# A fused attention and mixture-of-experts block on one Trainium2 core: the expert part rebuilt around one-hot bias matmuls, rows kept in place and pieces copied whole

## The reference

```python
x = x + xcond(layernorm(x), ctx, ctx, tau, delta, Wq, bq, Wk, bk, Wv, bv, Wo, bo)
# the FFN of the layernorm of that x:
logits = x @ router_w + router_b;  top1 = argmax(softmax(logits))
for i in range(8):
    h = x @ w1[i] + b1[i]                 # 256 -> 2 * 1024
    a, g = split(h, 2)
    y = (a * sigmoid(g)) @ w2[i] + b2[i]  # 1024 -> 256
    out = out + where(top1 == i, y, 0)
x = x + out
```

## Time and profile before

| | |
|---|---|
| three timed runs | 442.26, 443.79, 444.25 us; median 443.79 us |
| span of the profiled execution, first to last instruction | 441.3 us |
| the profiled execution's own time | no other than the span is shown; the median lies 2.5 us above it |
| TensorE matmul busy | 390.7 us (89%) |
| vector engine, ScalarE, GpSimd busy | 275.3, 236.1, 156.4 us |
| attention up to the routing | 0 to about 187 us |
| expert part | 207.4 us to the end |

### The profile page before, as it was taken

The page is one execution under the profiler, slowest core; times in us unless marked ns, Lnnn a source line. Parts: engine busy times, 40 slices in busy tenths (PEclk is TensorE's granted clock), DMA queues, the critical chain, the costliest instruction groups (busy, mean ns, idle before and its releaser), DMA issues.

```text
span 441.3 us, 8739 instructions
## 1 busy us (share of the span) xinstructions
PE 390.7 (89%) x2905; PEld 267.0 (61%) x2913; DVE 275.3 (62%) x734; ACT 236.1 (54%) x433; POOL 156.4 (35%) x195
## 2 busy tenths in 40 slices
PE   6959889898998889969887779989999999999990
PEld 3535444455564455735565667767697668968870
DVE  3859975577675754773635655476656567458750
ACT  3215567456465466103476775566675557657640
POOL 5349050011010010346776732142222235057742
PEclk9989999899998899996999998999999999999996
DMA  6655595261011562043785630393106911021311
GB/s 216 118 163 118 116 177 183 54 143 51 3 49 50 180 253 97 30 169 102 268 260 202 233 121 24 126 394 127 25 24 244 376 28 25 25 61 62 95 61 36
DMA packets 27042, 56.12 MB, mean 127 GB/s; under 512 B 6930, under 2 KB 17174, under 8 KB 26870
## 3 DMA queue, kind: packets, MB, share of 16 engines
q1 hardware_dynamic: 20954, 41.41, 29.7%
q0 software_dynamic: 4528, 13.16, 9.7%
q10 hardware_dynamic: 1516, 0.99, 1.0%
HBM read 41.23 MB, written 6.88 MB: 109 GB/s over the span
## 4 chain that ended last, share of the span: by engine, by line
PE 65%; DVE 11%; ACT 6%; issue 6%; DMA 5%; ACTq 1%; SPq 1%; POOL 1%; another core or an unknown queue 1%; DVEq 0%; POOLq 0%
PE bank L1242 17%; PE bank L1270 8%; PE bank L1235 7%; PE bank L1264 4%; PE bank L1082 4%; PE bank L1005 4%; DMA bias_in<-b_rows,bias_row 3%; PE bank L995 3%; DVE row_max L1601 3%; PE bank L944 2%; PE bank L905 2%; PE bank L881 2%; PE bank L1057 2%; PE bank L983 2%; ACT probs L1355 2%
## 5 line engine op out<-in xcount | busy, mean ns | idle before, releaser
L1242 PEld LDWEIGHTS bank<-slot_xt,w_now 128*128 128x128 f32 x832 | 100.4, 192 | 5.1 <-issue 2.0
L1242 PE MATMUL bank<-slot_xt,w_now 128*128 128x128 f32 x832 | 101.1, 275 | 2.1 <-issue 1.5
L826 POOL COPY piece_w<-w_sb 128x1024 f32 x30 | 31.6, 1060 | 97.4 <-PE bank L1235 97.3
L1601 DVE TENSOR_REDUCE row_max<-bank 128x3 f32<-128x462 f32 (+1 forms) x96 | 52.8, 579 | 17.0 <-PE bank L944 16.7
L1871 DVE SCALAR_TENSOR_TENSOR act_ut<-bank,b_of,gate 128x128 f32<-128x128 f32 x104 | 31.6, 346 | 50.0 <-ACT gate L1473 46.5
L1355 ACT ACTIVATE probs<-bank 128x512 f32<-128x512 f32 x80 | 45.9, 598 | 25.9 <-PE bank L983 17.0
L1445 ACT ACTIVATE w_now<-w_sb 128x1024 f32 x52 | 54.6, 1053 | 9.4 <-issue 9.3
L1270 PE MATMUL bank<-w_sb,act_ut 128*128 x208 | 55.2, 389 | 0.5 <-issue 0.5
L693 POOL TENSOR_SCALAR var<-mv 128x1 f32<-128x1 f32 (+1 forms) x20 | 4.5, 226 | 133.4 <-DVE mv L1638 109.5
L1901 DVE COPY piece_w<-w_sb 128x512 f32 x80 | 51.0, 658 | 1.3 <-issue 0.7
L1457 ACT ACTIVATE piece_w<-w_sb 128x1024 f32 x44 | 45.9, 1051 | 2.3 <-issue 2.3
(11 more groups left out here) (188 smaller groups left out, 575.9 us busy)
## 6 DMA issues: line engine op xcount, KB each, us to landing
w_sb<-in_weights_dram SPq DMA_DIRECT2D x32, 768.0 KB, 7.1
q_stack<-q_split SPq DMA_DIRECT2D x18, 256.0 KB, 5.2
rows<-row_buf SPq DMA_DIRECT2D x17, 256.0 KB, 2.2
x_sb<-in_x_dram SPq DMA_DIRECT2D x4, 512.0 KB, 6.2
b_sb<-in_b_dram SPq DMA_DIRECT2D x1, 1024.0 KB, 8.3
k_stack<-k_split SPq DMA_DIRECT2D x12, 77.0 KB
q_stack<-q_split ACTq DMA_DIRECT2D x6, 128.0 KB, 2.9
q_stack<-q_split SPq DMA_DIRECT2D x6, 128.0 KB, 2.7
```

Of the source, the lines that this page charges most:

```text
L1242: ins = pe.matmul(h_ps[j % RING][:, P * m:P * (m + 1)], w1_now[:, whole_count(n) % 2, k, P * m:P * (m + 1)], slot_xt[:, tile_at(n), k, :], ...
L1601: dve.tensor_reduce(row_max[:, c % 2, m, t, first:first + k], score_bank(c, i)[:, 0:k * CTX].rearrange("p (h s) -> p h s", s=CTX), AX_X, A ...
```

## The change

- Mixed tiles stand at 2, 5, 8, 11, 14, and the `down` of a mixed tile runs three steps after its `up`.
- b1 and b2 are split into three bf16 parts (`split_biases`, GpSimd, at step (0, 8)), stored and loaded back as `b_split`, 24 rows (3 parts x 8 experts). A one-hot `of_tile` picks the expert. Each mixed `up` begins with four bf16 matmuls of 24 rows x 32 columns x 512; in the first quarter each whole `down` begins with one of 24 x 128 x 256, and each mixed `down` with four of 24 x 32 x 256. The bias add on the vector engine, the gathers of b1 and b2 rows, `start_y`, `hidden`, `y_acc` and the 1 MB broadcast of b2 go.
- The transpose of b1 that feeds the split is moved from after the attention to step (0, 4) of TensorE (`turn_b1`), its copy to (0, 6) of ScalarE; `turn_x(3)` also waits for the copy.
- All 18 row gathers are issued one after another into `slot_rows`, where the turned rows are written back over the gathered ones and the outputs add up.
- Mixed pieces are copied whole, w1 and w2 together (1536 columns), into one of two sets: two by the vector engine, one by ScalarE, one by GpSimd, from three steps before their tile. A set is free when the mixed tile two back has had its `down`.
- The whole tiles' b1 columns of a quarter are placed by one masked product and one sum on the vector engine (`place_b1`), one quarter before the loop, three at steps 6, 9 and 12.

```diff
-MIXED_AT = (3, 6, 9, 12, 15)
+MIXED_AT = (2, 5, 8, 11, 14)
+MIXED_LAG = 3
+TURN_B1, SPLIT_BIASES = (0, 4), (0, 8)
...
+            def load_biases():
+                sp.wait_ge(pv_done, UNITS * CHUNKS)
+                sp.wait_ge(bias_stored, 32)
+                for w in range(PARTS):
...
             load_q(2)
             load_k(1)
             sp.dma_start(b1_sb[:, :, :], b1.rearrange("p (e m) -> p e m", m=HIDDEN_BLOCKS)).then_inc(s_b1, 16)
+            sp.dma_start(biases[:, P:], b2.rearrange("(p n) -> p n", p=P)).then_inc(s_b2, 16)
...
+            def turn_b1():
+                pe.wait_ge(s_b1, 16)
+                pe.wait_ge(q_low, KD)
+                pe.transpose(work_ps[0][:, 0:P], b1_sb[:, :, :].rearrange("p e m -> p (e m)"), ident).then_inc(b1_turned, 1)
...
+                if (c, i) == TURN_B1:
+                    turn_b1()
                 if c + 1 < CHUNKS:
                     scores(c + 1, i)
...
+            pool.wait_ge(tables_done, 1)
+            copy_piece(0)
             pool.wait_ge(routed, 1)
...
-            for j in range(GATHERS):
+            for j in range(SLOT_TILES):
                 gather(j)
+                if j == 5:
+                    copy_piece(1)
...
+                    for c in range(PIECES):
+                        pe.matmul(h_ps[j % RING][PIECE * c:PIECE * (c + 1), :], expert_rows(piece_at(k_mixed, c), PIECE),
+                                  b_split[:, 2 * HQ * q:2 * HQ * (q + 1)], start=True, stop=False, skip_group_check=True)
...
+                    if first:
+                        pe.matmul(y_ps[d % RING][:, 0:DIM], expert_rows(tile_at(n), P), b2_rows, start=True, stop=False)
...
+            def copy_piece(k, c):
+                at = piece_at(k, c)
+                wait_piece(dve, k)
+                if k < MIXED_TILES:
                     load_expert(at)
+                dve.tensor_copy(piece_w[:, k % 2, c, :], piece_weights(k, experts[at])).then_inc(pieces_dve, 1)
```

More of the change, by code:

```diff
@@ L99 @@
 BUSY_BEFORE_REST, BUSY_BEFORE_ROOMS, BUSY_BEFORE_FFN = 10, 2, 18
-GATHERS = 4
 RING = 3
@@ L328, in build @@
         zeros_stored = sem("zeros_stored")
-        gathered = [sem(f"gathered{n}") for n in range(GATHERS)]
+        gathered = [sem(f"gathered{n}") for n in range(SLOT_TILES)]
         s_out = sem("s_out")
@@ L466, in whole_at @@
             return [i for i in range(QUARTERS * SLOT_TILES) if not mixed(i)][w]
[L468 to L472, removed]
         def downs(n):
-            first = [last_mixed(n)] if mixed(n) and last_mixed(n) is not None else []
+            first = [n - MIXED_LAG] if n >= MIXED_LAG and mixed(n - MIXED_LAG) else []
             return first, [n - 2] if n >= 2 and not mixed(n - 2) else []
@@ L480, in build, with pieces_due, piece_at, wait_piece @@
         down_order = sum((sum(downs(n), []) for n in range(steps_all)), [])
-        down_order += [last_mixed(steps_all), steps_all - 2, steps_all - 1]
+        down_order += [steps_all - 2, steps_all - 1]
         def downs_before(n):
             return down_order.index(n)
[L487 to L510, removed]
+        def pieces_due(n, lag):
+            k = mixed_count(n - lag) if n >= lag and mixed(n - lag) else 0
+            return [k] if 2 <= k < QUARTERS * MIXED_TILES else []
+        def piece_at(k, c):
+            return WHOLE_TILES + PIECES * (k % MIXED_TILES) + c
+        def wait_piece(engine, k):
+            engine.wait_ge(s_quarter[k // MIXED_TILES], 16 * EXPERTS)
+            if k == 1:
+                engine.wait_ge(rest_ready, 1)
+            if k >= 2:
+                engine.wait_ge(y_ready, downs_before(mixed_at(k - 2)) + 1)
+        def piece_weights(k, expert):
+            return w_sb[:, bass.ds(k // MIXED_TILES % 2 * EXPERTS + expert, 1), :].rearrange("p o n -> p (o n)")
         def wait_gated(engine, n):
@@ L680, in _ @@
             for q in range(2, QUARTERS):
-                sp.wait_ge(y_ready, SLOT_TILES * (q - 1))
+                sp.wait_ge(y_ready, max(downs_before(n) for n in range(SLOT_TILES * (q - 2), SLOT_TILES * (q - 1)) if not mixed(n)) + 1)
                 load_experts(q, 0, EXPERTS)
@@ L860, in _ @@
             last_quarter = SLOT_TILES * (QUARTERS - 1)
             left = [n - last_quarter for n in down_order if n >= last_quarter]
[L862 to L866 removed]
+            for n in range(QUARTERS * SLOT_TILES):
+                for k in pieces_due(n, 0):
+                    copy_piece(k)
@@ L1258, in down @@
                 at = KD * 2 * HQ
+                first = n < SLOT_TILES
+                b2_rows = b_split[:, QUARTERS * 2 * HQ:]
                 if mixed(n):
-                    pe.wait_ge(ut_copied, mixed_count(n))
-                    pe.wait_ge(w2_copied, PIECES * mixed_count(n))
+                    k_mixed = mixed_count(n) - 1
+                    pe.wait_ge(ut_copied, k_mixed + 1)
+                    if first:
+                        for c in range(PIECES):
+                            pe.matmul(y_ps[d % RING][PIECE * c:PIECE * (c + 1), 0:DIM], expert_rows(piece_at(k_mixed, c), PIECE),
+                                      b2_rows, start=True, stop=False, skip_group_check=True)
                     for c in range(PIECES):
@@ L1893, in copy_w2 @@
-            def copy_w2(n, c):
-                q = n // SLOT_TILES
-                dve.wait_ge(s_quarter[q], 16 * EXPERTS)
-                if last_mixed(n) is not None:
-                    dve.wait_ge(y_ready, downs_before(last_mixed(n)) + 1)
-                at = WHOLE_TILES + PIECES * (tile_at(n) - WHOLE_TILES) + c
-                if q == 0 and experts[at] is None:
+                y = slot_rows[:, tile_at(n), DIM:2 * DIM]
+                dve.tensor_tensor(y, y_ps[d % RING][:, 0:DIM], y, ALU.add).then_inc(y_added, 1)
@@ L1904, in _ @@
             dve.wait_ge(s_b1, 16)
[L1905 to L1913 removed]
+            place_b1(0)
@@ L1914, in _ @@
+            for k in range(2):
+                for c in range(2):
+                    copy_piece(k, c)
             for n in range(QUARTERS * SLOT_TILES):
@@ L1917, in _ @@
                     add_y(i)
-                if mixed(n):
-                    bias(n)
-                for i, c in w2_pieces(n, False):
-                    copy_w2(i, c)
                 gated(n)
```

326 lines of the change are left out of this document (134 added, 192 removed).

## The result

The changed kernel takes 461.75 us (median of four runs, 461.19 to 469.15), the kernel before beside it 444.02 us (442.26 to 444.50). The ratio is 1.041, with a 95% interval of 1.038 to 1.045; the run of 469.15, in a second and slower state of the chip, is left out of it. The forecast was 459.6 and slower. The profiled execution took 461.21 us with a span of 459.4, against 441.3 before: 18.1 us more.

What follows compares the result with a forecast made beforehand. TensorE's stream was taken as the bound. Attention +16.3, start +0.2, first quarter -4.1, later quarters +3.7 and end -0.3 gave +15.8 on the 441.3 span: 457.1, with 2.5 for timed runs 459.6 us, range 451 to 468.

Steps and rivals of the forecast that it cites:

- The stall at (0, 4): Attention: TensorE waits at the moved b1 transpose from 53.4 to 68.3 for the b1 load, +14.9 us.
- The sum in the attention, +16.3: Attention: stall +14.9, transpose and copy +0.3, caught up -0.6, lower clock +1.7; between +13.4 and +19.2 us.
- Clock: Attention: after the pause TensorE again starts at its lower clock level, +1.7 us, between 0 and 3.4.
- The stall's own steps: Attention: wait for b1 +14.9, place of transpose and copy +0.3, part of TensorE's idle time caught up -0.6 us.
- the prediction's own sign: Profile after: L881 to L995 shifted by some 16 us until the routing, which begins near 203 in place of 187.
- The first quarter, -10.7 + 6.6 = -4.1: Experts' first quarter: TensorE's waits for pieces and lost clock go, -10.7 us; new bias matmuls cost +6.6.
- the one that named the gathers: First quarter: GpSimd and vector engine slow each other on pieces and 18 gathers, most of 10.7 stays; 467.6 us, chance 0.06.
- The size of a bias group, 0.40 taken: Experts: bias matmuls before a mixed up cost 0.40 us, a whole down 0.28, a first-quarter mixed down 0.20.
- the rival's high ends: Bias matmuls: every change of shape is paid twice, +3.9 and +2.7 us, total 466.2; chance 0.13.
- Later quarters, +3.7: Other three quarters: bias groups +6.0 us, idle time in the weight-loading stretches gone -2.3.
- The first piece of the next quarter: Quarter's end: it needs all eight weight loads two steps before the end; counted 0, up to +3 us.
- The end, -0.3: End of the experts: the last three steps are whole ones, -0.3 us.

Runs made afterwards that it cites:

- experiment 5: The changed kernel with early bias loads, row gathers held in step with TensorE and bias operands padded to 128 rows, run again: 435.63 us, ratio 0.976 to the kernel before.

## Why the prediction was right, and where it was not

**The stall at (0, 4): right, and shown from both sides.** The wait is 14.85 us in the kernel before with this edit alone, 13.39 in the changed one, and its removal gives 13.3 us between two kernels on the first chip. On the second chip the changed kernel stands 12.7 to 14.7 above the two with the early loads and a landing wait, the landing waits' own share included.

**The sum in the attention, +16.3: too high.** The profile after has +7.5 at the first row transpose, the same kernel's second profile +8.2. The step that failed is "Clock": after the stall it charged +1.7 on top of everything the kernel before loses. In place of that, the half-clock stretches lie elsewhere. Both profiles have 20.5 us of them before the first row transpose: the kernel before at 28 to 31, 79 to 83, 141 to 148 and 199 to 206, the changed one at 53 to 70 and 200 to 203. But 13.3 of the latter fall on the stall itself, where there is no work to slow. At half the clock 20.5 us lose 10.2 and the 7.2 that are left 3.6, an estimate of 6.6 us from these rows. The stall's own steps gave 14.6 up to the third activation transposes and the shift there is 12.85 (72.79 against 59.94), since the load came 1.5 us earlier. From there it melts to 9.4 at the last router matmul and 7.5 at the first row transpose, 5.4 us in all, which the clock is enough to explain; no run holds the clock fixed, so that is not shown. By the prediction's own sign the routing was to begin some 16 us later, near 203; it begins 9.4 us later. (The upper bound given for this sum, +19.2, is 18.9 by its terms.) How much melts differs between profiles: with the transpose moved alone in the kernel before, the first row transpose comes 13.0 us later; with the early loads, seven profiles (all but that of experiment 5) have it between 6.0 us earlier and 0.2 us later.

**The first quarter, -10.7 + 6.6 = -4.1: near where there is no hole.** From the first row transpose to down(17) it is 72.6 us before, and 69.2 in the kernel with the early loads and four gathers under way: -3.4.

```profile
201.20:217.00 15.80, 15.07 (x125) 11.61 (x127) 4.33 (x11) 8.26 (x20) 11.55 (x12) 1.00 0.85 285
217.00:270.40 53.40, 52.33 (x437) 37.56 (x429) 25.43 (x58) 30.02 (x59) 12.42 (x10) 1.00 0.34 114
```

The first quarter is the sum of the two windows. Waits for pieces have shrunk from 2.09 to between 0.34 and 0.40. With three under way it is +1.4, with the one late piece. In the changed kernel it is +8.8 on the first result and +0.1 on the second chip, with the wait for gather 4 and the half-clock stretch. That TensorE could stand still during the gathers was no rival of mine in this form; the one that named the gathers had them slow down copies.

**The size of a bias group, 0.40 taken: 0.44.** A whole `down` with its bias is 0.21 + 1.06 in the chain (L1260, L1262) against the 0.86 of the earlier trace rows, so 0.41 where 0.28 was taken; the bias ahead of a mixed `down` is 0.22, taken 0.20. Together 8.6 in the first quarter (6.6 forecast) and 6.6 in the others (6.0): the bias cost more than its middle, and less than the rival's high ends. The page "TensorEngine Tiling (Array Packing)" of the Trainium skill, section "Tiling Modes", says that a change of mode drains the engine. The trace agrees in kind: a group pays at both of its ends, some 0.11 us each. The padded kernel beside the unpadded one shows that a change in the number of operand rows is enough, with the same 32 columns.

**Later quarters, +3.7: +3.6.** The second and third quarters are 52.8 us each, against 52.0 and 51.7, the last one 49.6 against 47.9, and no wait in the weight-loading stretches is left. The first piece of the next quarter is not late.

**The end, -0.3: -1.8.** From the last `down` to the end of the span 8.7 us in place of 10.5.

**Why the total was right.** In part by luck. On the first result: attention 9.0 less than forecast, first quarter 12.9 more, end 1.5 less: +2.3 with the rounding. Without the hole, as on the second chip, the change costs 9.3 us, not 15.8, and the forecast of 459.6 would have been 7 us high, though within its range. The forecast's sign rested on the stall, and it holds in both measurements of the changed kernel. With the stall gone it turns: 0.987 with the gathers held.

**What stays open.** Why TensorE's signals came late on the first chip. Shown: the hole ends as the last gather lands; on that chip holding the gathers, with the piece copies moved in between, removes it; on the other chip it doesn't appear in any version; landing records are missing in the profiles of the first result and in all of the first chip, with a hole or without. So missing records alone don't make a hole. One profile of the unaltered kernel on each side is little to tell a chip from its state. The page "NOTIFIC — the notification-queue block" of the Trainium skill, section "Overflow: three behaviours, one of which stalls the engine", says that a full record queue, by its setting, loses records or stalls the engine that writes them. It has these as alternatives for one queue, while both signs stand together here, and no run here shows the mechanism. Nor does one show whether the hole would be there without a profile. The early loads with unbroken gathers were not run on the second chip, so it is not known what the landing waits by themselves cost or save there.

## What to carry to other kernels

Where a step is moved up in the stream of the bound engine, look up what it waits for in the queue that brings it: here one small load behind twelve others cost some 13 us, and a load issued some 21 us earlier (41.7 in place of 62.7) is most of what makes the change worth having. Give a small operand as many rows as its neighbours have; zero rows cost one memset of 2.08 us on GpSimd, and the change of shape costs 0.22 of the 0.44 us of each group. Before an edit is credited with removing a loss, run the unedited kernel on the same chip; landing waits, spacing and padding here all "removed" a hole that the unedited kernel doesn't have on that chip.

## What the runs showed of the hardware

- The same program took 461.75 us at first and 452.59 on a second chip, while the kernel before took 444.02 and 443.28. Of the 9.2 us between them 8.7 lie in the first quarter of the experts in the profiles, where one has the hole.
- The granted clock drops to its lower level (1.2 of 2.4 GHz) in stretches at the same work, in other places in each profile. Seven profiles with the early loads have the last router matmul between 183.5 and 188.6 us. The four at 183.5 to 184.3 have 3 to 7 us at the lower level before it, the three at 186.6 to 188.6 have 14 to 17. A difference of 5 us between single profiles is within this.
- A bias group (four bf16 matmuls of 32 columns) with operands of 24 rows costs 0.44 us between products of 128 rows, and with operands of 128 rows 0.22: more rows, half the time.
